# A recurrent two-layer kernel on one core: the query rotation of the second layer's attention goes from VectorE to ScalarE, DMA and GpSimd

## What is computed

```python
x = x + _attention(_rmsnorm(x, g1), wq, wk, wv, wo)        # 16 query heads, 4 key heads, head size 16

def _rotate_half(x):
    x1, x2 = jnp.split(x, 2, axis=-1)
    return jnp.concatenate([-x2, x1], axis=-1)

q, k = q * cos + _rotate_half(q) * sin, k * cos + _rotate_half(k) * sin
k, v = jnp.repeat(k, 4, axis=1), jnp.repeat(v, 4, axis=1)
scores = jnp.where(causal, q @ k.T / 4, -jnp.inf)
out = softmax(scores) @ v                                  # then @ wo
```

## Time and profile before

| | us |
|---|---|
| median of 3 runs | 3822.15 |
| lowest, highest | 3817.26, 3822.64 |
| the profiled execution, its own time | 3821.25 |
| its span in the profile | 3819.5 |
| PE / VectorE / ScalarE / GpSimd busy in the span | 3452.4 / 2525.3 / 2159.4 / 1132.5 |

### The profile page before, as it was taken

One profiled execution on the slowest core, in us unless ns is written; L12 is line 12 of the kernel. 1 busy time (PEld: TensorE's weight loads), 2 busy tenths in 40 slices (PEclk: granted clock), 3 DMA queues, 4 the chain that ended last, 5 costly groups with the idle time before them and its releaser, 6 DMA issues. The chain is left out here.

```text
span 3819.5 us, 68115 instructions
## 1 busy us (share of the span) xinstructions
PE 3452.4 (90%) x19130; PEld 2626.0 (69%) x19130; DVE 2525.3 (66%) x7151; ACT 2159.4 (57%) x5034; POOL 1132.5 (30%) x1770
## 2 busy tenths in 40 slices
PE   2999999999999999989999968868988885799996
PEld 2777777777777777768888844435666655688885
DVE  5777777777777777766666633346666645566665
ACT  1777777777777777755556531115455441355553
POOL 1333333333333333343343310021111100343442
PEclk9999999999999999989999977778899895899998
DMA  4222222222221222243343310010000004355454
GB/s 158 44 48 48 48 47 44 48 48 48 48 47 44 48 48 48 48 148 112 126 137 121 132 55 28 33 43 11 17 17 18 17 25 152 123 141 136 120 140 150
DMA packets 174565, 278.23 MB, mean 73 GB/s; under 512 B 31474, under 2 KB 118258, under 8 KB 174450
## 3 DMA queue, kind: packets, MB, share of 16 engines
q1 hardware_dynamic: 159858, 256.83, 23.2%
q0 software_dynamic: 14592, 19.93, 3.2%
HBM read 161.89 MB, written 41.16 MB: 53 GB/s over the span
## 5 line engine op out<-in xcount | busy, mean ns | idle before, releaser
L723 POOL TENSOR_SCALAR at_p<-at_p,at_recip 128x128 f32<-128x128 f32 (+3 forms) x1028 | 533.6, 531 | 983.5 <-DVE at_recip L862 983.5
L773 ACT ACTIVATE at_p<-at_p,at_nmax 128x128 f32<-128x128 f32 (+3 forms) x1030 | 575.7, 559 | 291.0 <-DVE at_nmax L856 287.8
L856 DVE CUSTOM_DVE_ANT_0 at_p<-at_s_ps,at_bias 128x128 f32<-128x128 f32 (+3 forms) x1030 | 493.3, 479 | 154.8 <-PE at_s_ps L971 154.8
L978 PE MATMUL at_t_ps<-ident,at_p 128*128 128x128 f32 x2560 | 459.7, 278 | 0.4 <-POOL at_p L723 0.4
L970 PE MATMUL at_s_ps<-at_k_twice,at_q 128*128 128x128 f32 (+3 forms) x1030 | 387.9, 377 | 7.8 <-DVE at_nmax L856 1.2
L1730 DVE CUSTOM_DVE_ANT_0 aa_a_ps<-aa_a_ps,aa_hidden 128x128 f32<-128x128 f32 (+3 forms) x512 | 247.2, 506 | 183.0 <-PE aa_a_ps L1900 179.4
L1628 ACT ACTIVATE aa_pT<-aa_b_ps 128x512 f32<-128x512 f32 (+1 forms) x384 | 197.0, 527 | 259.8 <-PE aa_b_ps L1918 256.1
L971 PE MATMUL at_s_ps<-at_k_twice,at_q 128*128 128x128 f32 (+3 forms) x1030 | 332.1, 322 | 0.0
L978 PEld LDWEIGHTS at_t_ps<-ident,at_p 128*128 128x128 f32 x2560 | 294.9, 140 | 46.4 <-DVE at_pT L869 30.0
L988 PE MATMUL at_o_ps<-at_pT,at_v 128*64 128x512 f32 (+3 forms) x2064 | 306.3, 439 | 0.0
L988 PEld LDWEIGHTS at_o_ps<-at_pT,at_v 128*64 128x64 f32 x2064 | 136.7, 136 | 175.8 <-issue 156.9
(11 more groups left out here) (315 smaller groups left out, 8683.5 us busy)
## 6 DMA issues: line engine op xcount, KB each, us to landing
at_k_twice<-at_k_parts SPq DMA_DIRECT2D x260, 256.0 KB, 3.3
nw_w_raw<-in_w_all_dram SPq DMA_DIRECT2D x52, 1024.0 KB, 7.4
w_raw<-in_w_dram SPq DMA_DIRECT2D x57, 768.0 KB, 5.8
ln_x<-in_x_dram SPq DMA_DIRECT2D x10, 512.0 KB, 4.5
nw_xh<-xh_dram SPq DMA_DIRECT2D x10, 512.0 KB, 4.4
nw_xl<-xl_dram SPq DMA_DIRECT2D x10, 512.0 KB, 4.9
rc_x<-x_dram SPq DMA_DIRECT2D x10, 512.0 KB, 3.8
at_w_raw<-in_w_heads_dram SPq DMA_DIRECT2D x18, 256.0 KB, 3.4
```

The lines of the kernel that those rows point to most:

```text
L723: pool.tensor_scalar(p, p, recip[:, u:u + 1], 1.0, ALU.mult, ALU.mult).then_inc(scaled, 1)
L773: act.activation(p_sb[:, u, 0:N], p_sb[:, u, 0:N], ACT.Exp, bias=nmax[:, u:u + 1], scale=-1.0, accum_out=total[:, u:u + 1]).then_inc(exped, 1)
L856: dve.tensor_tensor_reduce(out=p_sb[:, u, 0:N], in0=s_ps[u % 2][:, 0:N], in1=bias[:, u % 2, S - N:S], scale=1.0, scalar=BIG, op0=ALU.add, ...
L978: ins = pe.transpose(t_ps[u % 2][:, k * P:k * P + P], p_sb[:, u, k * P:k * P + P], ident[:])
```

## The change

VectorE no longer takes q0, q1, x0 and x1. ScalarE takes x0 and x1 (`take_x`, with the scale g1) and copies q0, q1 unchanged into `turn1` (`take_raw`). SP copies the four blocks of 32 partitions, neighbours exchanged, from `turn1` to `turn2` by four DMAs of 64 KB (`exchange`), between `place` and `pack`. POOL makes the two products with cos and sin ahead of its five instructions, now seven, and the table of sines is laid out for the exchanged rows. k0 goes from slot (3, 0) to (4, 0). `make_xr` makes its four parts at the ends of steps 11, 12, 14 and 15, each waiting for the half of the queries whose slot it overwrites. The rest of the diff follows the counts of semaphores.

```diff
@@ -1368,7 +1368,7 @@
     cos, sin = np.cos(angle).astype(np.float32), np.sin(angle).astype(np.float32)
     sin[:QD // 2] *= -1.0
     d = q_features()[0:P] % QD
-    cos_q, sin_q = cos[d], sin[(d + QD // 2) % QD]
+    cos_q, sin_q = cos[d], sin[d]
     cos, sin = np.tile(cos, (P // QD, 1)), np.tile(sin, (P // QD, 1))
     k_table = np.concatenate([cos[:P // 2], sin[:P // 2]])
     return np.ascontiguousarray(np.stack([-0.25 * cos_q, -0.25 * sin_q, k_table], 1).astype(np.float32))
@@ -1442,6 +1442,7 @@
         made = sem("aa_made")
         dve_out = sem("aa_dve_out")
         act_out = sem("aa_act_out")
+        exchanged = sem("aa_exchanged")
         q_turned = sem("aa_q_turned")
         k_turned = sem("aa_k_turned")
         k_low = sem("aa_k_low")
@@ -1463,7 +1464,7 @@
         block = ctx.enter_context(nc.Block())
         GROUPS = B * KV1
         FIRST = ["x0", "x1", "kk", "q0", "k0", "p0", "p1", "v", "q1", "k1", "p2", "p3", "M0", "k2", "k3", "p4", "p5", "p6", "p7"]
-        NEXT = {(0, 0): "x0", (0, 1): "x1", (1, 1): "kk", (2, 0): "q0", (3, 0): "k0", (3, 1): "v", (4, 1): "p0", (5, 1): "p1",
+        NEXT = {(0, 0): "x0", (0, 1): "x1", (1, 1): "kk", (2, 0): "q0", (4, 0): "k0", (3, 1): "v", (4, 1): "p0", (5, 1): "p1",
                 (6, 0): "k1", (7, 1): "p2", (9, 1): "p3", (10, 0): "q1", (10, 1): "k2", (11, 0): "k3", (12, 1): "p4",
                 (13, 0): "M0", (13, 1): "p5", (14, 0): "p6", (15, 0): "p7"}
         SAME = {(1, 0): "M1", (5, 0): "M2", (9, 0): "M3"}
@@ -1486,7 +1487,7 @@
                 ORDER.extend(job for job in (side_job(n, s, 0), side_job(n, s, 1)) if job)
         ORDER.extend((B - 1, name) for name in ("out0", "out1"))
         PLACE = {job: i for i, job in enumerate(ORDER)}
-        BY_ACT = [name[0] in "Mkp" and name != "kk" for _, name in ORDER]
+        BY_ACT = [name[0] in "Mkpqx" and name != "kk" for _, name in ORDER]
 
         def bank_of(n, name):
             return m_ps[PLACE[n, name] % 2]
@@ -1518,6 +1519,13 @@
                     for g in range(KV1):
                         sp.dma_start(k_all[i][at:at + QD, e, g, :].bitcast(F32), ones).then_inc(ones_placed, 16)
 
+            def exchange(n, m):
+
+                sp.wait_ge(act_out, out_by(PLACE[n, f"q{m}"]))
+                for block in range(4):
+                    to, of = QUARTER * block, QUARTER * (block ^ 1)
+                    sp.dma_start(turn2[to:to + QUARTER, m, :], turn1[of:of + QUARTER, m, :]).then_inc(exchanged, 16)
+
             def place(G):
 
                 n, g = divmod(G, KV1)
@@ -1549,11 +1557,17 @@
                 sp.dma_start(shares[low:low + 64, :], recip_dram[G % 2].rearrange("(h a) c -> h a c", a=1)
                              .broadcast_to([REP, QD, S])).then_inc(shares_in, 16)
 
+            exchange(0, 0)
+            exchange(0, 1)
             place(0)
             place(1)
+            exchange(1, 0)
             for G in range(GROUPS):
                 if G + 2 < GROUPS:
                     place(G + 2)
+                n, g = divmod(G + 1, KV1)
+                if g % 2 == 0 and n + 1 < B:
+                    exchange(n + 1, g // 2)
                 pack(G)
                 spread_out(G)
             sp.wait_ge(loaded, 32)
@@ -1593,20 +1607,23 @@
                 pool.wait_ge(k_turned, 2 * n + 2)
 
             def turn_q(n, m):
-                count = 10 * n + 5 * m
+                count = 14 * n + 7 * m
                 low, high = slice(0, P // 2), slice(P // 2, P)
-                pool.wait_ge(dve_out, out_by(PLACE[n, f"q{m}"]))
+                pool.wait_ge(exchanged, 64 * (2 * n + m + 1))
+                pool.tensor_tensor(turn1[:, m, :], turn1[:, m, :], rope[:, 0, :], ALU.mult).then_inc(q_turned, 1)
+                pool.tensor_tensor(turn2[:, m, :], turn2[:, m, :], rope[:, 1, :], ALU.mult).then_inc(q_turned, 1)
+                pool.wait_ge(q_turned, count + 2)
                 pool.tensor_tensor(turn1[:, m, :], turn1[:, m, :], turn2[:, m, :], ALU.add).then_inc(q_turned, 1)
-                pool.wait_ge(q_turned, count + 1)
+                pool.wait_ge(q_turned, count + 3)
                 pool.tensor_scalar(q_parts[low, m, 0, :], turn1[low, m, :], 1.0, 1.0, ALU.mult, ALU.mult).then_inc(q_turned, 1)
                 pool.tensor_scalar(q_parts[high, m, 1, :], turn1[high, m, :], 1.0, 1.0, ALU.mult, ALU.mult).then_inc(q_turned, 1)
-                pool.wait_ge(q_turned, count + 3)
+                pool.wait_ge(q_turned, count + 5)
                 pool.tensor_tensor(q_parts[high, m, 0, :], turn1[low, m, :], q_parts[low, m, 0, :].bitcast(F32), ALU.subtract)\
                     .then_inc(q_turned, 1)
-                pool.wait_ge(q_turned, count + 4)
+                pool.wait_ge(q_turned, count + 6)
                 pool.tensor_tensor(q_parts[low, m, 1, :], turn1[high, m, :], q_parts[high, m, 1, :].bitcast(F32), ALU.subtract)\
                     .then_inc(q_turned, 1)
-                pool.wait_ge(q_turned, count + 5)
+                pool.wait_ge(q_turned, count + 7)
 
             turn_k(0)
             turn_q(0, 0)
@@ -1639,6 +1656,15 @@
                 act.wait_ge(made, made_by(n, f"p{i}"))
                 act.activation(q_all[n % 2][:, i, :], bank_of(n, f"p{i}")[:], ACT.Copy).then_inc(act_out, 1)
 
+            def take_x(n, k):
+
+                act.wait_ge(made, made_by(n, f"x{k}"))
+                act.activation(xrT[:, k, :], bank_of(n, f"x{k}")[:], ACT.Copy, scale=g1_sb[:, k:k + 1]).then_inc(act_out, 1)
+
+            def take_raw(n, m):
+                act.wait_ge(made, made_by(n, f"q{m}"))
+                act.activation(turn1[:, m, :], bank_of(n, f"q{m}")[:], ACT.Copy).then_inc(act_out, 1)
+
             def take_minus(n, g):
                 act.wait_ge(made, made_by(n, f"M{g}"))
                 if n * KV1 + g > 0:
@@ -1653,6 +1679,10 @@
                 act.activation(o_sb[:], o_ps[:], ACT.Copy).then_inc(o_out, 1)
 
             def take(job):
+                if job and job[1][0] == "x":
+                    take_x(job[0], int(job[1][1]))
+                if job and job[1][0] == "q":
+                    take_raw(job[0], int(job[1][1]))
                 if job and job[1][0] == "M":
                     take_minus(job[0], int(job[1][1]))
                 if job and job[1][0] == "k" and job[1] != "kk":
@@ -1660,6 +1690,7 @@
                 if job and job[1][0] == "p":
                     take_q(job[0], int(job[1][1]))
 
+            act.wait_ge(loaded, 32)
             for name in FIRST:
                 take((0, name))
             late = None
@@ -1680,18 +1711,11 @@
         def _(dve):
             low, high = slice(0, P // 2), slice(P // 2, P)
 
-            def make_xr(n):
+            def make_xr(n, i):
                 if n > 0:
-                    dve.wait_ge(q_turned, 10 * n)
-                for i in range(TT):
-                    dve.tensor_scalar(xr[:, i, :], y[:, n * TT + i, :], r1[:, n * TT + i:n * TT + i + 1], None, ALU.mult)\
-                        .then_inc(xr_made, 1)
-
-            def take_x(n, k):
-
-                dve.wait_ge(made, made_by(n, f"x{k}"))
-                dve.tensor_scalar(xrT[:, k, :], bank_of(n, f"x{k}")[:], g1_sb[:, k:k + 1], None, ALU.mult)\
-                    .then_inc(dve_out, 1)
+                    dve.wait_ge(q_turned, 14 * (n - 1) + 7 * (i // 2) + 7)
+                dve.tensor_scalar(xr[:, i, :], y[:, n * TT + i, :], r1[:, n * TT + i:n * TT + i + 1], None, ALU.mult)\
+                    .then_inc(xr_made, 1)
 
             def take_k(n):
                 dve.wait_ge(made, made_by(n, "kk"))
@@ -1703,15 +1727,6 @@
                 dve.wait_ge(made, made_by(n, "v"))
                 dve.tensor_copy(v[n % 2][:, :, :, 0:QD], bank_of(n, "v")[:, 0:TT * KV1 * QD]
                                 .rearrange("p (i g d) -> p i g d", g=KV1, d=QD)).then_inc(dve_out, 1)
-
-            def take_q(n, m):
-                dve.wait_ge(made, made_by(n, f"q{m}"))
-                bank = bank_of(n, f"q{m}")
-                dve.tensor_tensor(turn1[:, m, :], bank[:], rope[:, 0, :], ALU.mult)
-                for block in range(4):
-                    to, of = slice(QUARTER * block, QUARTER * block + QUARTER), slice(QUARTER * (block ^ 1), QUARTER * (block ^ 1) + QUARTER)
-                    ins = dve.tensor_tensor(turn2[to, m, :], bank[of, :], rope[of, 1, :], ALU.mult)
-                ins.then_inc(dve_out, 1)
 
             def low_k(n):
                 dve.wait_ge(k_turned, 2 * n + 2)
@@ -1759,42 +1774,36 @@
                 if not job:
                     return
                 n, name = job
-                if name[0] == "x":
-                    take_x(n, int(name[1]))
                 if name == "kk":
                     take_k(n)
                 if name == "v":
                     take_v(n)
-                if name[0] == "q":
-                    take_q(n, int(name[1]))
                 if name[0:3] == "out":
                     take_out(n, int(name[3]))
 
-            make_xr(0)
```

(21 more changed lines are left out.)

## The result

The changed kernel took 3857.53 us (median of 4 runs, 3855.60 to 3862.18), the kernel before 3819.70 on the same chip (median of 4, 3816.36 to 3822.64): a ratio of 1.0101 with an interval of 1.0084 to 1.0119. The forecast was 3878 in a range from 3835 to 3900, slower by over 0.2% at 0.85. The direction and the range held; the size was +38 us where +57 stood. The profiled execution took 3857.93 us (span 3856.1).

What follows compares the result with a forecast made beforehand. TensorE bounds the kernel, busy 63 to 64 of 72 us per batch. Per batch -1.6 (p0), +2.7 (p4) and +7.0 (slow clock) make +8.1, times 7 = +57; 3821 + 57 = 3878, range 3835 to 3900.

Steps and rivals of the forecast that it cites:

- The waits of before go: PE's 2.72 and 1.15 us waits behind q0 and 2.48 behind q1 vanish; maxima's waits fall from 47.6 to some 11.
- The chain of 15.6 us: Rotation through ScalarE's copy, SP's four DMAs and POOL's instructions is ready 15.6 us after q0, and likewise after q1.
- -1.6 and +2.7 of the sum: Per batch, p0 starts 15.6 us after q0 instead of 17.2; p4 15.6 after q1 instead of 12.9.
- PE comes after 9.0 us: PE would reach p0 and p4 9.0 us after their q, so stand about 6.6 us at each.
- the "90 us" of waits: Sign of being right: 14 PE waits for POOL of 6 to 7 us, some 90 us where 0.5 stood.
- The slow stretch behind each wait: Low clock after p0 and p4, 6.8 to 10.2 us, mid 8.5, costing 3.8 each: +7.0 net per batch.
- The price of 0.45 us per slow us: Factor for PE's low clock throughout the sum: each slow us costs 0.45 us.
- The first rival, 3850: Waits come, but about 4 us of slow clock remain after each, 1.8 lost each: +29, 3850; chance 0.14.
- The rival without any fall: Waits come with no clock fall at all: 7 x 1.1 = +8, 3829; chance 0.04.
- the forecast's own bounds of 3862 to 3898: Spread around 3878 from slow stretches of 6.8 to 10.2 us, 11 either way, and from DMA landings.
- The first batch: Chain at the start ends 2.8 us later, partly regained behind q1: net +0.5, between -3 and +3.
- Faster: Rotation ready before PE comes at p0 and p4, so waits and slow clock go: -98, 3723; chance 0.11.

Runs made afterwards that it cites:

- The first two orders: Changed kernel with k1 ahead of p0 and p0 to p3 later: 3807.36 us; then also q1 in (8, 1), p3 in (10, 0), exchange ahead of place: 3777.12 us.
- the third: Changed kernel with the edits of both earlier orders, and p4 moved from (12, 1) to (13, 1), p5 to (14, 0), p6 to (14, 1): 3745.44 us, ratio 0.9803.
- the kernel with the longer chain: Changed kernel with one more 128 x 512 POOL product in each rotation, into a tile nobody reads: 3875.07 us, ratio 1.0147.
- the series above: Three successive reorderings of jobs and DMAs in the changed kernel: 3807.36, 3777.12, 3745.44 us; the waits of 2.0 to 2.2 us are the second's.
- the last kernel with VectorE's pieces: Kernel before, VectorE's rotation in five parts between the maxima, side jobs reordered, p2, p3, k2, k3 half a step later still: 3792.18 us, ratio 0.9922.

## Why the prediction was right in kind and 20 us too high

**The waits of before go: right.** The 2.72, 1.15 and 2.48 us are gone but for 0.47, and the maxima's waits fell from 47.6 us to 22.6 over the same 500 us. The expectation of 11 was too low: new ones of 0.4 to 1.6 us stand just ahead of p0 and p4, where they cost nothing, since PE then waits for POOL anyway. One batch shows it: ahead of its p4 (2726.15) no such wait stood, PE came 1.8 us sooner and waited 6.9 us instead of 4.8.

**The chain of 15.6 us: right, link by link.** Copy, four issues in 2.43 us for 2.46, landing 2.0, POOL's products 1.27 and p0 at 15.56, p4 at 15.68. -1.67 and +2.78 stand for the -1.6 and +2.7 of the sum. The Trainium skill (DMA: Bandwidth & Descriptors, Anatomy of one DMA) gives the fixed part of about 2.0 us for DMAs that GpSimd issues; these are issued by SP, and the trace agrees with it all the same. The 64 KB landed after 2.0 us like the 32 KB of the earlier trace rows, so the estimated 0.08 us more doesn't show in a figure of one decimal.

**PE comes after 9.0 us: off, but outside the sum.** It came after 11.0 us at p0 and 10.9 at p4 in thirteen cases of fourteen, so a wait is 4.6 to 4.8 us, not 6.6; only in the batch named above it came after 9.1. The new waits make up 1.1 us of the 11.0 and 2.2 of the 10.9 (1.55 of them the maxima ahead of p4). At p0 I had also taken the clock's gain and the waits off in full: 1.0 of the 9.7 slow us lay inside the 1.15 us wait. The last half us is not placed. As p0's time is set by the chain, the sum doesn't contain this number; the "90 us" of waits does, and was 67.6.

**The slow stretch behind each wait: the term that was mis-sized.** "After a longer wait I expect the clock down once more for about as long as the rows show, 6.8 to 10.2 us, mid 8.5", all behind p0 and p4: +7.0 net of what stood there before. The stretches are 6.8 and 10.2 us long, as said, but 1.7, 3.4 and 4.1 us of the three shown lie inside the wait, and 5.1, 3.4 and 6.1 behind it; over all 14 the mean behind it is 4.7. The table has +2.07 and +1.46 in the two segments, +3.5 for the +7.0. With 4.7 in place of 8.5 the sum's own working gives 7 x (1.1 + 2 x 4.7 x 0.45 - 0.6) = +33, for +35.2 at p7 of the last batch (3121.64, before 3086.42) and +36.7 between the profiled executions. The price of 0.45 us per slow us held in this batch: 2.07 us for 4.6 more slow us is 0.45, 1.46 for 3.1 is 0.47 (0.5 and 0.4 stood there before; PE's other waits are the same in the first segment and 0.16 us longer in the second, which would make it 0.42). The first rival, 3850, said this in kind; its 4 us of rest and the forecast's 8.5 bracket what came, nearer to the rival. Its argument, that the fall had come within 0.5 us of the wait's end and so may lie inside a longer wait, was in the trace of before and should have had the larger chance: the falls came 0.6 to 2.9 us after the wait began. The rival without any fall forgot to take off the 0.6 that stood behind p0 and p4 before; by the sum's own terms it is 7 x 0.5 = +4, not +8. Nor do the forecast's own bounds of 3862 to 3898 follow from the terms named for them: 11 us either way and landings of 1.9 to 3.7 us (-1 to +24) would make 3866 to 3913.

**The first batch: right.** -0.5 us where +0.5 stood, within its -3 to +3, though the wait before its p0 is 9.22 us where 4.43 stood: p0 starts 2.2 us later there (2556.78 for 2554.55), and the rest of the batch gives that back.

**Faster: ruled out by the change as it stands, and reached by moving the jobs around it.** The rival put the turning point at a chain under 9 us; the other way round it is PE's coming after 15.6. The first two orders do that for p0, the third for both, and 3745 is the result. The forecast for that case, 3723, was 22 lower. The waits show about half of it: 14.6 us for the maxima where 11 were to remain, 3.6 at the transposes and 3.3 for ScalarE's exps, both new. The rest is not placed.

## What to carry to other kernels

When work moves from one engine to a chain over several, measure the chain from its source to its user against the time until the user comes, and move the user's job as late as its banks allow in the same edit: here the same change is 1% slower or 2% faster by the order of jobs and DMAs alone. Count a wait of TensorE with the slow clock behind it, but only the part of the slow stretch that outlives the wait. An engine's relief can be tested for its worth by hiding all that was added, as the version of 3745 us does.

## What the runs showed of the hardware

**GpSimd holds up small instructions of VectorE.** VectorE makes the negated maxima of a group in two tiny instructions, 176 and 178 ns in the median. Where they start behind one of POOL's products they take up to seven times as long. VectorE's timeline, then POOL's, ahead of p4:

```profile
2796.11 1.24 DVE L1754 TENSOR_SCALAR aa_minus<-aa_nmax 128x16 fp32r<-128x16 f32 x1
2797.38 1.19 DVE L1756 SCALAR_TENSOR_TENSOR aa_minus<-aa_nmax,aa_minus 128x16 fp32r<-128x16 f32 x1
2798.49 0.29 DVE L1745 CUSTOM_DVE_ANT_0 aa_a_ps<-aa_a_ps,aa_hidden 128x128 f32<-128x128 f32 x1
```

```profile
2795.91 1.40 POOL L1613 TENSOR_TENSOR aa_turn<-aa_turn,aa_rope 128x512 f32<-128x512 f32 x1 [31.15 <-DMA aa_turn<-aa_turn]
2797.28 1.26 POOL L1614 TENSOR_TENSOR aa_turn<-aa_turn,aa_rope 128x512 f32<-128x512 f32 x1
2798.61 1.27 POOL L1616 TENSOR_TENSOR aa_turn<-aa_turn 128x512 f32<-128x512 f32 x1
```

L1754 ends at 2797.35 and L1756 at 2798.57, each within 0.05 us of the end of a POOL product (2797.31 and 2798.54), and the next maxima, which read PSUM, start only then: that is the wait of 1.55 us in PE's timeline. It is so ahead of six of the seven p4. Ahead of the seventh both started before POOL's first product (2718.10), took 0.17 and 0.18 us, and PE's wait for the maxima isn't there. The kernel before has it smaller: one of the two took 0.43 to 0.70 us in seven groups, each time up to the end of a POOL instruction. In the kernel with the longer chain the same happened ahead of p0. VectorE, then POOL, of that kernel:

```profile
2769.46 1.18 DVE L1758 SCALAR_TENSOR_TENSOR aa_minus<-aa_nmax,aa_minus 128x16 fp32r<-128x16 f32 x1
```

```profile
2769.36 1.26 POOL L1616 TENSOR_TENSOR aa_spare<-aa_rope 128x512 f32<-128x512 f32 x1
```

Its 0.18 us became 1.18, and the maxima's waits grew by the 6.3 us told above. The Trainium skill (SBUF — State Buffer, SBUF: two separate sides) describes the ports that VectorE and GpSimd share as an exclusive lock, held for a whole instruction, against VectorE instructions with two inputs in SBUF or in a two-port mode. L1756 has two such inputs and agrees, with 1.19 us; L1754 has one, and fits only if it runs in such a mode, which no run here shows. A VectorE engine that is 54% busy (215.49 of the 400 us above) can so be late by POOL's doing.

**Short waits can bring the slow clock.** In the series above seven waits of 2.0 to 2.2 us were followed by 3.4 us at 1.2 GHz, once by 6.8. In the last kernel with VectorE's pieces shorter ones were. Three windows and PE's timeline of that kernel:

```profile
2665.00:2670.00 5.00, 2.94 (x20) 2.33 (x18) 4.82 (x12) 2.02 (x5) 0.00 (x0) 0.98 0.13 28
2670.00:2675.00 5.00, 5.00 (x21) 4.71 (x20) 3.24 (x12) 1.12 (x3) 3.81 (x4) 0.50 0.00 0
2700.00:2705.00 5.00, 4.71 (x29) 3.24 (x29) 2.52 (x10) 1.96 (x4) 4.29 (x5) 0.66 0.00 1
```

```profile
2667.07 0.38 PE L1922 MATMUL aa_a_ps<-aa_k,aa_q 128*128 128x256 f32 x1 [0.71 <-DVE aa_nmax L1737]
2668.79 0.45 PE L1922 MATMUL aa_a_ps<-aa_k,aa_q 128*128 128x384 f32 x1 [1.16 <-DVE aa_nmax L1737]
...
2699.66 0.30 PE L1922 MATMUL aa_a_ps<-aa_k,aa_q 128*128 128x128 f32 x1 [1.41 <-DVE aa_nmax L1737]
```

Waits of 0.71 and 1.16 us within 3 us were followed by a stretch that begins at 2669.8, and one of 1.41, with 0.33 right behind it, by 3.4 us. But the length of a wait doesn't settle it. The fastest kernel has this one, and ran at 2.4 GHz from 2600 to 2650 us as over the 400 us behind:

```profile
2611.30 0.44 PE L1911 MATMUL aa_a_ps<-aa_k,aa_q 128*128 128x384 f32 x1 [1.30 <-DVE aa_nmax L1747]
2600.00:2650.00 50.00, 46.40 (x303) 31.67 (x301) 35.56 (x132) 33.64 (x67) 17.12 (x16) 1.00 0.11 26
```

And in the kernel before the 2.48 us behind one q1 brought no fall, while the same wait in the batches around it did. What makes the difference no run here shows.
